# Every 64th chunk of a row gather fetched row by row by SyncE instead of by one GpSimd indirect DMA

## The reference

```python
# x: node features after layer 0, shape (6250, 128)
edge_input = concat(x[src], x[dst])                       # 100000 x 256
message    = gelu(edge_input @ eW1 + eb1) @ eW2 + eb2
aggregated = segment_sum(message, dst, 6250)
x = layernorm(x + x + mlp(concat(x, aggregated)))
```

## Time and profile before

| | us |
|---|---|
| median of 3 runs | 2852.22 (2851.33 to 2857.69) |
| the profiled execution, its own time | 2850.75 |
| its span, first to last instruction | 2849.1 |
| gather stage, first row-number DMA to last use of a_rows | 1788.3 to 2778.8 |
| mean granted TensorE clock | 0.975 |

### The profile page before, as it was taken

The page is one execution under the profiler, slowest core; times in us unless marked ns, Lnnn a source line. Parts: engine busy times, 40 slices in busy tenths (PEclk is TensorE's granted clock), DMA queues, the critical chain, the costliest instruction groups (busy, mean ns, idle before and its releaser), DMA issues. The chain is left out here.

```text
span 2849.1 us, 92390 instructions
## 1 busy us (share of the span) xinstructions
PE 2465.8 (87%) x23996; PEld 2171.2 (76%) x23997; DVE 1922.8 (67%) x9459; ACT 1006.4 (35%) x2286; POOL 1857.9 (65%) x2595
## 2 busy tenths in 40 slices
PE   7778888888888888799999989788888888998997
PEld 6568777777777777477777766688888888898997
DVE  8678777777777777677778777444455555555556
ACT  7334333333333333144444447222222222222225
POOL 1047777777777777654444447677777777777764
PEclk9789999999999999899999999999999999999999
DMA  5021111111111111188889972222222222222221
GB/s 186 29 56 47 45 45 46 45 45 46 45 45 45 46 45 50 46 220 226 227 224 228 226 182 70 54 54 54 54 54 54 53 54 54 54 54 54 54 50 46
DMA packets 582005, 236.12 MB, mean 83 GB/s; under 512 B 512257, under 2 KB 553773, under 8 KB 581677
## 3 DMA queue, kind: packets, MB, share of 16 engines
q1 hardware_dynamic: 298020, 98.53, 15.3%
q0 software_dynamic: 52736, 93.92, 11.8%
q10 hardware_dynamic: 231176, 42.79, 7.4%
HBM read 142.39 MB, written 98.65 MB: 85 GB/s over the span
## 5 line engine op out<-in xcount | busy, mean ns | idle before, releaser
L1041 POOL DMA_INDIRECT edge_in_src_order<-u,place x784 | 754.7, 963 | 261.9 <-issue 185.1
L1714 POOL DMA_INDIRECT a_rows<-src_table,idx x782 | 742.7, 950 | 255.4 <-issue 237.1
L1411 POOL COPY m_s<-m 128x144 f32 x832 | 233.0, 323 | 245.3 <-PE ps_pre L1458 244.7
L1814 ACT ACTIVATE h<-ps_h 128x512 f32<-128x512 f32 x208 | 124.2, 597 | 758.4 <-PE ps_h L1786 660.4
L1759 DVE TENSOR_SCALAR ohd_f<-iota_b,dloc_c 128x128 f32<-128x128 bf16 x832 | 185.9, 291 | 260.8 <-PE ps_n L1796 256.8
L1795 PE MATMUL ps_s<-ohd_f,h 128*128 128x128 f32 x1664 | 359.4, 306 | 0.0
L1747 DVE TENSOR_TENSOR hsumT<-hsumT,ps_s 128x128 f32 x832 | 239.4, 288 | 156.6 <-issue 67.9
L1781 PE MATMUL ps_h<-a_rows,ident 128*128 x1664 | 240.3, 288 | 114.4 <-SPq L1723 98.1
L1434 DVE TENSOR_TENSOR_SCAN top<-same,top,ps_net 96x512 f32<-96x512 bf16 x207 | 264.1, 1276 | 97.9 <-PE ps_net L1465 97.6
L1258 PE MATMUL ps_u<-we_s,attrT 128*128 128x384 f32 x392 | 173.9, 525 | 158.6 <-ACT u L1335 158.6
L1335 ACT COPY u<-ps_u 128x384 f32<-128x384 f32 x196 | 93.7, 478 | 603.0 <-DMA edge_in_src_order<-u,place 586.2
(11 more groups left out here) (356 smaller groups left out, 5472.0 us busy)
## 6 DMA issues: line engine op xcount, KB each, us to landing
u_in<-edge_in_src_order SPq DMA_DIRECT2D x208, 192.0 KB, 3.3
running_max<-row ACTq DMA_DIRECT2D x208, 192.0 KB, 4.1
rowt<-src_row SPq DMA_DIRECT2D x208, 130.0 KB, 3.7
key_b<-edge_keys ACTq DMA_DIRECT2D x832, 1.5 KB
edge_in_src_order<-u,place POOLq DMA_INDIRECT x784, 2.2
a_rows<-src_table,idx POOLq DMA_INDIRECT x782
edge_attributes<-in_edge_attr SPq DMA_DIRECT2D x8, 784.0 KB, 12.3
attr_in<-edge_attributes SPq DMA_DIRECT2D x196, 32.0 KB, 1.9
```

The costliest lines, as they stand in the source:

```text
L1041: pool.indirect_dma_start(u_d, bass.IndirectOffsetOnAxis(place[:, u, j:j + 1], 0), ur[:, u, j, :], None).then_inc(sent[u], 16)
L1411: last = nc.gpsimd.tensor_copy(m1_s[:, u, j, :], m1[:].bitcast(F32)[:, bass.ds(at[j], 3 * F // 2)])
L1714: pool.indirect_dma_start(a_rows[:, 4 * u + j, :], None, a_d, bass.IndirectOffsetOnAxis(idx[:, u % 4, j:j + 1], 0)).then_inc(got[u % 4], 16)
```

## The change

Chunks 63, 127, ..., 767 (ASIDE = 12 chunks) are no longer fetched by GpSimd. SP fetches them with one DMA per row: 8 rows in each of its turns 0 to 191, so 16 turns per chunk, into two extra places behind the ring. The row numbers reach SP's registers through a table `aside` in one partition of SBUF, made in two steps by way of HBM in the scan and table stages. slot_row is changed so that TensorE looks for these chunks in the two extra places. The unroll of SP's and GpSimd's pipelines goes from 8 to 32, so SP's turns 0 to 95 are written out straight, 96 to 191 are three rounds of a loop of 32, and 192 to 203 come after.

```diff
+    ASIDE = NC // 64
+    aside_d = nc.dram_tensor("rows_fetched_one_by_one", (P, ASIDE), I32).ap()
...
# scan stage, SP, behind the loads
+                        sp.wait_ge(aside_set, 1)
+                        sp.dma_start(aside_d, aside_c[:]).then_inc(aside_out, 16)
+                        sp.wait_ge(aside_out, 16)
# scan stage, DVE
+                        v.tensor_copy(aside_c[:], src_c[:, 63:64 * ASIDE:64]).then_inc(aside_set, 1)
                         pipeline(dve, G, [(4, scan), (0, onehot)])
+                        ch = Chain(dve, slot_chain)
+                        v.tensor_single_scalar(odd_64[:], e0_row[:], 64, op=ALU.bitwise_and)
+                        ch(v.tensor_single_scalar(of_64[:], e0_row[:], 63, op=ALU.bitwise_and))
+                        v.tensor_scalar(odd_64[:], odd_64[:], float(D) / 64, float(D), ALU.mult, ALU.add)
+                        ch(v.tensor_scalar(of_64[:], of_64[:], 63.0, None, ALU.is_equal))
+                        ch(v.tensor_tensor(odd_64[:], odd_64[:], of_64[:], ALU.mult))
+                        v.tensor_tensor(slot_row[:], slot_row[:], odd_64[:], ALU.add)
# table stage, SP
+                        sp.dma_start(aside[:], aside_d.rearrange("e t -> (e t)").unsqueeze(0)).then_inc(aside_in, 16)
...
+                        sp.wait_ge(aside_in, 16)
# gather stage
-                a_rows = sb(t, "a_rows", [P, 4 * RING, D])
+                a_rows = sb(t, "a_rows", [P, 4 * RING + 2, D])
...
-                            for j in range(4 if not isinstance(g, int) else min(4, NC - 4 * g)):
-                                pool.indirect_dma_start(a_rows[:, 4 * u + j, :], None, a_d,
+                            for j in range(min(3 if u % 16 == 15 else 4, NC - 4 * g if isinstance(g, int) else 4)):
+                                pool.indirect_dma_start(a_rows[:, 4 * (u % RING) + j, :], None, a_d,
...
-                        pipeline(pool, CG, [(0, fetch)], cool=1, unroll=RING)
+                        pipeline(pool, CG, [(0, fetch)], cool=1, unroll=32)
...
+                            less = 16 * (4 * CG - NC) if last else 0
+                            if u % 4 == 3:
+                                less += 16 * ((u + 1) // 16)
+                            sp.wait_ge(got[u % 4], (480 if u % 4 == 3 else 512) * n + 64 * (u // 4 + 1) - less)
+                            if u % 16 == 15:
+                                pass_waits(sp, passed_sp)
+                                sp.wait_ge(aside_got[u // 16], 16 * P * (n + 1))
                             sp.sem_inc(landed, 1)
...
+                        def one_by_one(g, u, n):
+                            if isinstance(g, int) and g >= 16 * ASIDE:
+                                return
+                            for r in range(8 * (u % 16), 8 * (u % 16) + 8, 4):
+                                at = offsets(nc, mybir.EngineType.SP, aside[0:1, :].rearrange("a (e t) -> a t e", t=ASIDE)[0:1, bass.ds(2 * n + u // 16, 1), r:r + 4], NP - 1)
+                                for j in range(4):
+                                    sp.dma_start(a_rows[r + j:r + j + 1, 4 * RING + u // 16, :], a_d[bass.ds(at[j], 1), :]).then_inc(aside_got[u // 16], 16)
-                        pipeline(sp, CG, [(4, all_here), (RING, used_up), (0, indices)], cool=1, unroll=RING)
+                        pipeline(sp, CG, [(4, all_here), (RING, used_up), (0, indices), (0, one_by_one)], cool=1, unroll=32)
```

More of the change, by code:

```diff
@@ L1389, in gnn @@
                 row_out = [sem(t, f"row_out{k}") for k in range(4)]
+                slot_chain = sem(t, "slot_chain")
+                aside_set = sem(t, "aside_set")
+                aside_out = sem(t, "aside_out")
+                aside_c = sb(t, "aside_c", [P, ASIDE], I32)
+                of_64 = sb(t, "of_64", [1, NS], I32)
+                odd_64 = sb(t, "odd_64", [1, NS], I32)
                 with nc.Block() as block:
@@ L1502, in gnn @@
             hsumT = sb(layer1, "hsumT", [D, NP])
+            aside = sb(layer1, "aside", [1, P * ASIDE], I32)
             deg = sb(layer1, "deg", [P, NB])
@@ L1550, in gnn @@
                 combined = sem(t, "combined")
+                aside_in = sem(t, "aside_in")
                 halved = sem(t, "halved")
@@ L1697, in gnn @@
                 got = [sem(t, f"got{k}") for k in range(4)]
+                passed_sp = sem(t, "passed_sp")
+                aside_got = [sem(t, f"aside_got{k}") for k in range(2)]
                 passed = sem(t, "passed_d")
@@ L1709, in fetch @@
                         def fetch(g, u, n):
-                            pool.wait_ge(idx_in[u % 4], 16 * (2 * n + u // 4 + 1))
+                            pool.wait_ge(idx_in[u % 4], 16 * (8 * n + u // 4 + 1))
                             wait(pool, freed, g - (RING - 1))
                             pass_waits(pool, passed)
-                            for j in range(4 if not isinstance(g, int) else min(4, NC - 4 * g)):
-                                pool.indirect_dma_start(a_rows[:, 4 * u + j, :], None, a_d,
+                            for j in range(min(3 if u % 16 == 15 else 4, NC - 4 * g if isinstance(g, int) else 4)):
+                                pool.indirect_dma_start(a_rows[:, 4 * (u % RING) + j, :], None, a_d,
                                                         bass.IndirectOffsetOnAxis(idx[:, u % 4, j:j + 1], 0)).then_inc(got[u % 4], 16)
-                        pipeline(pool, CG, [(0, fetch)], cool=1, unroll=RING)
+                        pipeline(pool, CG, [(0, fetch)], cool=1, unroll=32)
                     @block.sync
@@ L1721, in all_here @@
                             last = isinstance(g, int) and g == CG - 1
-                            sp.wait_ge(got[u % 4], 64 * (2 * n + u // 4 + 1) - (16 * (4 * CG - NC) if last else 0))
+                            less = 16 * (4 * CG - NC) if last else 0
[5 more added lines that the diff above has]
+                                sp.wait_ge(aside_got[u // 16], 16 * P * (n + 1))
                             sp.sem_inc(landed, 1)
@@ L1731, in indices @@
                             sp.dma_start(idx[:, u % 4], src_c[:, bass.ds(4 * g, 4)]).then_inc(idx_in[u % 4], 16)
-                        pipeline(sp, CG, [(4, all_here), (RING, used_up), (0, indices)], cool=1, unroll=RING)
+                        def one_by_one(g, u, n):
[5 more added lines that the diff above has]
+                                    sp.dma_start(a_rows[r + j:r + j + 1, 4 * RING + u // 16, :], a_d[bass.ds(at[j], 1), :]).then_inc(aside_got[u // 16], 16)
+                        assert 16 * ASIDE == (CG - 1) // 32 * 32
+                        pipeline(sp, CG, [(4, all_here), (RING, used_up), (0, indices), (0, one_by_one)], cool=1, unroll=32)
                     @block.vector
@@ L1776, in pre @@
                             here = offsets(nc, mybir.EngineType.PE, land_row[0:1, bass.ds(i, 1)], CG)
-                            slot = offsets(nc, mybir.EngineType.PE, slot_row[0:1, bass.ds(4 * i, 4)], (4 * RING - 1) * D)
+                            slot = offsets(nc, mybir.EngineType.PE, slot_row[0:1, bass.ds(4 * i, 4)], (4 * RING + 1) * D)
                             pe.wait_ge(landed, here[0])
```

## The result

The changed kernel takes 3215.9 us (median of 3 runs, 3214.5 to 3216.1) where the kernel before takes 2852.2: ratio 1.127, 95% interval 1.1255 to 1.1287. The direction and the mechanism were forecast, the size was not: +363.7 us instead of +54, outside the range.

A forecast was written before the change was run, and what follows sets the result against it. GpSimd's fetches were taken to bound the gather stage, with SP becoming the bound after the change. Later last fetch 48, tail 6 and scan stage 0.3 made 54 us on 2850.75, 2905, put at 2906 for the median; range 2862 to 3005.

The forecast's parts named there:

- the wait at line 1723: SP's wait for gathers to land in the gather stage: to fall from 592 us to near nothing.
- TensorE's wait for SP: Gather stage, named as a sign: to grow from 98 us to over 150.
- A row: One single-row DMA on SP with its address work: taken as 0.425 us, eight per turn 3.40 us.
- the signs named beforehand: What the changed profile should show, among them idx DMAs in the gather stage starting 5.0 to 5.6 us apart.
- The tail: End of the gather stage, TensorE's last steps after the last fetch: 6 us more, counted from 7.
- DVE's six operations: On a row of 832 at the scan stage's end: some 4.0 us, of which 0.3 us would show.
- the 0.5 us named as a sign: The scan stage should end within 0.5 us of where it did.
- Register loads: SP's two loads of four values per turn: 0.35 us each, together 0.70 straight and 0.88 in the loop.
- the 1012 summed: SP's turns 0 to 191 with row work: 1014.7 us, less about 3 us for the first eight turns.
- 10 us outside its sum for longer code: Fetching SP's and GpSimd's longer straight code while they run: some 10 us kept on the upper side.
- loads near 0.42: SP's register loads at 0.42 instead of 0.32 us: +38 us on the main sum; no chance of its own.
- it does what it is built to do: SP's turn fits under GpSimd's 4.92 us, fetches stay the bound, time falls by 15 to 2837 us; chance 0.09.

The follow-up runs named there:

- k5: Changed kernel with packed table, one load of eight per turn, one row-number DMA per four groups, free_row four at a time, eight gather semaphores: 2838.3 us, ratio 0.9947.
- k2: Changed kernel with row numbers loaded once into four registers ahead of the stage and used for all 1536 row DMAs: 2837.0 us, ratio 0.9945.
- e1: Changed kernel without its 1536 row DMAs, both register loads meant to stay, in a slower set: 3842 us, one run.
- k3: Changed kernel with the table laid out chunk by chunk, so a load's four values lie side by side: 3000.2 us, ratio 1.052.
- k4: Changed kernel with the table laid out chunk by chunk and one load of eight values per turn instead of two of four: 2922.0 us, ratio 1.024.

## Why the prediction missed, step by step

**Right.** GpSimd was the bound and SP became it; the wait at line 1723 was used up; 12 fetches less; TensorE's wait for SP over 150 us (304). A row cost 0.41 us against 0.425. Of the signs named beforehand one failed by far: row-number DMAs start 6.55 and 6.93 us apart, not 5.0 to 5.6. The tail: from the last fetch to the last step with line 1781 (now 1821) 12.8 us against 7.3 in the earlier trace rows, +5.5 for the 6 summed. Its last row:

```profile
3141.48 1.14 PE L1821 MATMUL ps_h<-a_rows,ident 128*128 x8
```

DVE's six operations took 4.3 us against 4.0, and the scan stage ended 0.57 us later against 0.3, just outside the 0.5 us named as a sign (memset at 1700.74 beside the earlier trace rows):

```profile
1696.09 0.56 DVE L1451 TENSOR_SCALAR odd<-e_row 1x832 int32<-1x832 int32 x1
...
1699.35 1.01 DVE L1456 CUSTOM_DVE_ANT_0 slot_row<-slot_row,odd 1x1664 uint16<-1x1664 uint16 x1
1700.74 0.27 DVE L1672 MEMSET aggT<- 2x256 f32 x1 [0.38 <-PEq L1398]
```

**The step that failed** is the one that reads "Register loads. [...] I take 0.32 plus 0.03 to the next instruction, 0.35 us". The 384 loads of aside took 377 us where 123 were summed (0.32 each): +254. The same step left the load of free_row at its old price; it stands behind row DMAs now and took 87 us in all instead of 54: +33. Both come from one mistake: a price was taken from loads of values that lie side by side, with no DMA straight in front or with DMAs of 128 rows, and put on a load with another form (four values 48 bytes apart) and another neighbour. The diff said how the values lie, and I did not ask what the spacing costs.

**Smaller terms.** Of the 307 us by which 192 turns exceed the 1012 summed, 287 are the loads; the 49 gaps of 0.36 us add about 17, the two returns to the loop's head 6, the rows are 11 cheaper; 8 us are not assigned. The prediction kept 10 us outside its sum for longer code; no run shows that the gaps or the returns are that term. The stage began 2.5 us later than before, but the kernel before began it 1.9 us later too in its second profile, so I count only the 0.6 us of the scan stage to the change.

**The range** failed for the same reason. Its upper end came from the price of a row, which turned out right; the case "loads near 0.42" was +38 us and had no bound from above, though a load of 513 ns stood in the earlier trace rows and was left out as a first of its block. By the floor of about 600 ns that the Trainium skill gives ("DMA: Bandwidth & Descriptors", "Latency and other measured facts") the sum would have been 107 us higher, as an estimate 3013 us, nearer but still 203 us short. SP's loads measured 0.27 to 1.11 us in the medians, depending on form and neighbour, so the floor does not hold here.

**The rival "it does what it is built to do"** did not come about in this kernel, but k5 shows that its mechanism is right, and k2 with less work for a row: 2838 and 2837 us, where 2837 was worked out. The mean turn must come under 4.98 us; in the changed kernel it is 6.87. The mispriced loads are 1.5 us of these 1.9. Without them the turn would still have been some 0.4 us too long, so the forecast that the kernel gets slower did not hang on them, only its size did.

The Trainium skill says that spreading DMAs over the engines that can issue them may help where descriptor generation is the bottleneck ("Perfetto Trace Analysis", "DMA Optimizations"). The runs agree with that "may": +364 us with SP's turn at 6.87 us, and 15 us less in k5, where SP's turn fits.

## What to carry to other kernels

Before work is moved into another engine's idle time, write out that engine's turn with every instruction that comes along, addresses and register loads too, and set it against the budget. Beyond the budget the idle time is not free: here each 0.1 us over it cost 19 us. Price an instruction from a row of the same form and with the same neighbour, or measure it first. Here a register load of several values was cheaper by 0.56 us when it read them side by side, and by 0.16 to 0.25 us when it did not stand straight behind one-row DMAs. If the moved work does not fit, thin out what the engine did before: one load of eight, one DMA for four groups and free_row four at a time turned +364 us into -15. That gain is small, and in the slower sets it was a loss of 2%.

An experiment that holds a value fixed can remove more than it means to. In e1 the loads vanished with their use, and in k2 the address work went with them; count the instructions of the line in both traces.

## What the runs showed of the hardware

- SP's register load from SBUF, medians: 0.27 us for one value with no DMA straight in front (kernel before), 0.45 behind row DMAs; four values side by side 0.30 us behind the row-number DMA, 0.55 behind row DMAs (k3); four values 48 bytes apart 0.87 and 1.11 (changed kernel); eight side by side 0.53 (k4), behind row DMAs 0.69 (k5). Behind row DMAs with a register instruction between, as in the loop: 0.47 for four side by side and 1.03 for four apart.
- A DMA of one row of 512 bytes with an address from a register is issued in 225 ns (260 for the first behind a load), and another can follow every 0.41 us; every 0.32 us in k2, where the address is not computed anew.
- 1536 such DMAs beside the gathers did not slow a fetch: 945 ns in the median and 1.25 us apart in k2 and k5 as in the kernel before.
- In the changed kernel TensorE's granted clock in the middle of the gather stage fell from 1.00 to 0.86, a mix of its two levels (1.2 and 2.4 GHz), while its busy time in 850 us fell from 755 to 651 us. The columns are start and end of the stretch, its length, busy us (instructions) of PE, PEld, DVE, ACT and POOL, granted clock, DMA share, GB/s. First the kernel before, then the changed one. The matmuls of line 1821 became longer (332 ns instead of 288 in the mean), but TensorE waited 304 us for SP in this stage, so their length is not what set the time.

```profile
1890.00:2740.00 850.00, 754.95 (x6487) 741.01 (x6485) 443.77 (x2338) 193.42 (x361) 643.64 (x678) 1.00 0.29 54
```

```profile
1890.00:2740.00 850.00, 651.28 (x4679) 641.20 (x4678) 324.58 (x1689) 143.59 (x260) 465.62 (x492) 0.86 0.21 40
```

- In three of the sets the kernel before took 3804 to 3850 us instead of 2850 to 2855, and the traces of those sets show stops of the sequencers of some 0.7 us. The cause was not looked for.
